# A gated cross-attention layer on one core: two batches' keys and queries built ahead of the batch loop

## The reference, cut to what matters

```python
# x: (8, 112, 256)   ctx: (8, 375, 256)   16 heads of 16 channels   8 zones, top 3
def attention(queries, keys, values, mask):          # keys = values = ctx
    q, k, v = heads(queries @ Wq + bq), heads(keys @ Wk + bk), heads(values @ Wv + bv)
    scores = where(mask, -1e15, q @ k.T / sqrt(16))
    return (softmax(scores) @ v) @ Wo + bo

def ffn(x):
    w = top-3 shares of softmax(tanh(mean_rows(x) @ W1 + b1) @ W2 + b2)    # per batch
    return x + sum over zones e of w[e] * (gelu(x @ Wa[e]) @ Wb[e])        # Wa: 256x1024, Wb: 1024x256

x = x + tanh(g_xattn) * attention(layernorm(x), ctx, ctx, mask)
x = x + tanh(g_ffn) * ffn(layernorm(x))
```

## Time and profile before

| what | value |
|---|---|
| median of three runs | 325.48 us |
| profiled execution | 328.27 us, span on the core 326.4 us |
| PE, DVE, ACT, POOL busy | 88%, 69%, 68%, 41% of the span |
| first score tile of batch 0 (start of body -1) | 24.69 us |
| starts of bodies 0, 1, 2, 3, 4, 5 and 6 | 45.01, 65.80, 85.91, 107.63, 128.33, 148.46 and 168.74 us |
| first matmul of the zone passes | 202.44 us |

### The profile page before, as it was taken

How to read it: one execution, slowest core, us unless ns; L and a number is a source line. 1 busy time by engine, 2 the same in 40 slices (tenths; PEclk the granted TensorE clock), 3 DMA queues, 4 the chain that set the end, 5 groups by cost and what they waited for, 6 DMA issues and landing times.

```text
span 326.4 us, 10356 instructions
## 1 busy us (share of the span) xinstructions
PE 287.3 (88%) x3940; PEld 238.6 (73%) x3940; DVE 225.3 (69%) x642; ACT 223.1 (68%) x439; POOL 135.4 (41%) x185
## 2 busy tenths in 40 slices
PE   1808769899989999999998977899999999999996
PEld 1505546667756776767765646799999989999996
DVE  7326846657757797777867626876976877686773
ACT  2221456786958968789687674986866977766863
POOL 3401274876768968689677983000100000000000
PEclk9967989999999999999999999999999999999999
DMA  7457667686777778866686322100201011010101
GB/s 166 120 125 239 156 176 213 167 241 172 233 182 216 206 230 230 264 177 172 207 217 208 88 87 80 38 19 16 58 17 46 3 44 37 11 45 3 32 2 30
DMA packets 39457, 40.59 MB, mean 124 GB/s; under 512 B 10264, under 2 KB 35264, under 8 KB 39408
## 3 DMA queue, kind: packets, MB, share of 16 engines
q1 hardware_dynamic: 37296, 38.94, 42.5%
q10 hardware_dynamic: 1936, 0.79, 1.0%
q0 software_dynamic: 176, 0.20, 0.2%
HBM read 33.09 MB, written 6.74 MB: 122 GB/s over the span
## 4 chain that ended last, share of the span: by engine, by line
PE 63%; DMA 12%; ACT 7%; issue 6%; DVE 5%; SPq 4%; POOL 3%; DVEq 0%; ACTq 0%
PE bank L1280 16%; PE bank L1307 16%; PE bank L1119 7%; PE bank L1128 5%; PE bank L1069 4%; DMA qbd<-q_scr 4%; PE bank L1081 4%; DMA stage<-in_L_ffn_Wb 4%; PE bank L1085 3%; PE bank L1101 2%; ACT pT L555 2%; PE bank L1110 2%; PE bank L1145 2%; DMA ctx_s<-in_ctx 2%; POOL wa L474 1%
## 5 line engine op out<-in xcount | busy, mean ns | idle before, releaser
L807 DVE CUSTOM_DVE_ANT_0 bank<-bank,maskb 112x375 f32<-112x375 f32 x128 | 67.9, 571 | 42.1 <-PE bank L1069 42.1
L1280 PE MATMUL bank<-ctxT,wqkvo 128*128 128x112 f16 x960 | 59.4, 213 | 2.7 <-DVE qbd L933 2.3
L1280 PEld LDWEIGHTS bank<-ctxT,wqkvo 128*128 128x128 f16 x960 | 56.5, 98 | 3.4 <-issue 3.4
L1307 PE MATMUL bank<-stage,pT 128*128 128x112 f16 x1104 | 58.1, 213 | 0.0
L1307 PEld LDWEIGHTS bank<-stage,pT 128*128 128x128 f16 x1104 | 55.8, 98 | 0.3
L555 ACT ACTIVATE pT<-bank 125x448 f32<-125x448 f32 x96 | 49.0, 540 | 9.9 <-PE bank L1085 9.3
L469 POOL TENSOR_SCALAR stage<-stage 128x512 f32<-128x512 f32 x64 | 38.5, 620 | 27.4 <-DMA stage<-in_L_ffn_Wa 20.6
L1069 PE MATMUL bank<-kst,qbd 128*112 128x375 f16 x128 | 33.7, 338 | 16.0 <-DMA qbd<-q_scr 12.7
L474 POOL TENSOR_TENSOR wb<-stage,wb 128x512 f16<-128x512 f32 x32 | 37.6, 1195 | 14.5 <-ACT wb L665 14.4
L1081 PE MATMUL bank<-rq,maskb 115*128 115x448 bf16 (+1 forms) x96 | 35.5, 370 | 8.3 <-ACT pT L555 7.8
L474 POOL TENSOR_TENSOR wa<-stage,wa 128x512 f16<-128x512 f32 x32 | 36.4, 1158 | 10.8 <-ACT wa L665 10.8
(11 more groups left out here) (134 smaller groups left out, 480.2 us busy)
## 6 DMA issues: line engine op xcount, KB each, us to landing
stage<-in_L_ffn_Wa SPq DMA_DIRECT2D x16, 512.0 KB, 4.5
stage<-in_L_ffn_Wb SPq DMA_DIRECT2D x16, 512.0 KB, 4.5
kst<-k_scr SPq DMA_DIRECT2D x64, 93.8 KB, 3.6
k_scr<-wb SPq DMA_DIRECT2D x16, 187.5 KB
ctx_s<-in_ctx SPq DMA_DIRECT2D x8, 336.0 KB
qbd<-q_scr SPq DMA_DIRECT2D x32, 56.0 KB, 3.0
xa<-in_x SPq DMA_DIRECT2D x8, 112.0 KB, 4.1
q_scr<-wb SPq DMA_DIRECT2D x16, 56.0 KB, 3.3
```

What stands on the lines that cost most here:

```text
L807: v.tensor_tensor_reduce(out=bank[0:SQ, e, 0:SK], in0=bank[0:SQ, e, 0:SK], in1=maskb[0:SQ, b % 2, 0:SK], scale=-1.0, scalar=FLOOR, op0=ALU ...
L1280: ins = T.matmul(o, first(ws, t, f), x2b[:, b % 2, (xs * DT + t) * SQ:(xs * DT + t + 1) * SQ], start=(t == 0 and xs == 0 and ws == 0), sto ...
L1307: ins = T.matmul(o, second(u, ws * (2 * CHUNK) + f * D + t * 128), hT[:, u % 2, hs * FT * SQ + f * SQ:hs * FT * SQ + (f + 1) * SQ], start= ...
```

## The change

- The loop starts at b = -1. What the first body did, and what the second did for batch 1, stands ahead of the loop as straight code on every engine: contexts, keys and queries of batches 0 and 1 and the values of batch 0, in the order of the tuple `AHEAD` on PE. Body -1 then holds only the score maxima of batch 0.
- In body 0 the first `s1(1, 0)` stands ahead of `st_tile(0, 0, 0)`; in all others it stays behind.
- The queries of batches 0 and 1 are read back over POOL's queue (`read_q` takes the engine), and signal semaphores of their own.
- Of the small inputs and weights that ACT's queue loaded, the key and query biases go to SP's, Wo, bv and the gates to POOL's; Wk is asked for ahead of Wq. On ACT the scaling of Wq moves behind the first copies. Two of DVE's five memsets move to POOL.
- The 64 parts of the zones' weights are spread otherwise: none ahead of body 0 slot 1, two a slot from there on, four in slot 2 of bodies 2 and 4, the last two in slot 2 of body 7.
- PE makes 12 products that nothing reads at its start and two more behind XT of batch 0 (`busy`).

```diff
--- before.py
+++ after.py
@@ parts_at
-            n = min(2 if (i, j) >= (-1, 2) else 0, NPART - at)
+            n = min(0 if (i, j) < (0, 1) else 4 if (i, j) in ((2, 2), (4, 2)) else 2, NPART - at)
@@
+def made(b):
+
+    return b + 2 if b >= 0 else B
+
+
+AHEAD = (("CX0", 0), ("CX1", 0), ("XT", 0), ("K0", 0), ("Q", 0), ("K1", 0), ("V0", 0), ("V1", 0),
+         ("CX0", 1), ("CX1", 1), ("XT", 1), ("K0", 1), ("Q", 1), ("K1", 1))
@@ slot_uses
-    n, m, o = b + 1, b + 2, b - 1
+    n, m, o = b + 1, made(b), b - 1
...
-    more = {(B - 2, 3): ("H", 0), (B - 1, 0): ("L", 0), (B - 1, 2): ("W", 0), (-1, 3): ("BO", 0)}.get((b, slot))
-    return [u for u in every[slot] if there(u[1])] + ([more] if more else [])
+    more = {(B - 2, 3): ("H", 0), (B - 1, 0): ("L", 0), (B - 1, 2): ("W", 0), (0, 3): ("BO", 0)}.get((b, slot))
+    return [u for u in every[slot] if there(u[1]) and u not in AHEAD] + ([more] if more else [])
@@ sync
+            sp.dma_start(bk_c[:, :], bk.rearrange("(t p) -> p t", p=128), allow_slow_non_contiguous=True).then_inc(s["bk_loaded"], 16)
...
+            load_mask(0)
+            load_ctx(1)
+            load_x(1)
+            write_k(0, 0)
+            write_q(0)
+            write_k(0, 1)
+            read_k(0, 0)
+            load_mask(1)
+            read_k(0, 1)
+            write_k(1, 0)
+            write_q(1)
+            load_x(2)
+            write_k(1, 1)
+            load_ctx(2)
+            read_k(1, 0)
+            for b in range(-1, B):
+                n, m, o = b + 1, made(b), b - 1
+                if n > 1:
+                    read_k(n, 1)
+                    read_q(sp, n, 1)
...
+                if b == -1:
+                    read_k(1, 1)
                 read_k(m, 0)
-                read_q(m, 0)
+                read_q(sp, m, 0)
@@ gpsimd
-            pool.wait_ge(s["zeroed"], 5)
+            chain.link(g.memset(vp[:].rearrange("p a c h i -> p (a c h i)"), 1.0))
...
+            g.memset(pT[96:CK + 1, :, :], 1.0).then_inc(s["ones_ready"], 1)
+            pool.wait_ge(s["ones_ready"], 3)
+            norm1(1)
+            read_q(pool, 0, 0)
+            read_q(pool, 0, 1)
+            g.dma_start(wqkvo[:, 3, :, :], view_w(Wo)).then_inc(s["wo_loaded"], 16)
...
+            read_q(pool, 1, 0)
+            read_q(pool, 1, 1)
+            for b in range(-1, B):
@@ scalar
             normed(0)
+            cx_copy(0)
+            xt_copy(0)
             act.wait_ge(s["wq_loaded"], 16)
...
+            k_hi(0, 0)
+            q_hi(0)
+            k_hi(0, 1)
+            v_copy(0, 0)
+            normed(1)
+            v_copy(0, 1)
+            cx_copy(1)
+            xt_copy(1)
+            mask_bias(0)
+            k_hi(1, 0)
+            q_hi(1)
+            k_hi(1, 1)
+            mask_bias(1)
@@ vector
-            v.memset(pT[96:CK + 1, :, :], 1.0).then_inc(s["zeroed"], 1)
-            dve.wait_ge(s["zeroed"], 5)
...
+            cx_copy(0)
+            dve.wait_ge(s["bk_loaded"], 16)
+            k_lo(0, 0)
...
+            ln1_stats(1)
+            cx_copy(1)
+            k_lo(1, 0)
+            q_lo(1)
+            k_lo(1, 1)
@@ tensor
+            def busy(n):
+
+                for i in range(n):
+                    T.matmul(bank[:, ST_BANKS[i % 2], 0:128], ident[:, :], ident[:, :], start=True, stop=True)
...
-            pe.wait_ge(s["zeroed"], 3)
-            for b in range(-2, B):
+            busy(12)
+            for name in AHEAD:
+                put(name)
+                if name == ("XT", 0):
+                    busy(2)
+            for b in range(-1, B):
                 for slot in range(4):
-                    st_tile(b, slot, 0)
-                    s1(b + 1, 2 * slot)
+                    if (b, slot) == (0, 0):
+                        s1(1, 0)
+                        st_tile(0, 0, 0)
+                    else:
+                        st_tile(b, slot, 0)
+                        s1(b + 1, 2 * slot)
```

More of the change, by code:

```diff
@@ L92, in __init__ @@
     def __init__(self):
-        names, banks = [], []
-        for b in range(-2, B):
+        names = list(AHEAD)
+        banks = [MISC_BANKS[i % len(MISC_BANKS)] for i in range(len(AHEAD))]
+        for b in range(-1, B):
             for slot in range(4):
@@ L284, in full, with read_q @@
             eng.wait_ge(s["misc_full"], spare.full(name))
+        def read_q(eng, b, h):
+            if there(b):
+                eng.wait_ge(s["q_written"], b * 32 + 32)
+                need(eng, s["pe_st"], tile(b - 2, 2 * h + 2, 0))
+                need(eng, s["dve_max"], s1_no(b - 2, 4 * h + 4, 0))
+                run = PAIRS * SQ
+                for e in range(2):
+                    eng.dma_start(qbd[64 * e:64 * e + 64, b % 2, e, HP * h:HP * h + HP, :].rearrange("p j f -> p (j f)"),
+                                 bass.AP(q_scr.tensor, (b * DT + e) * (HD * 2 * run) + HP * h * SQ,
+                                         [[run, 2 * HD], [0, 2], [1, HP * SQ]])).then_inc(s["q_first%d%d" % (b, h)] if b < 2 else kq_in[b % 2][h], 16)
         block = stack.enter_context(nc.Block())
@@ L319, in write_k @@
                                  k_hl[:, t, :, :]).then_inc(k_written[t], 16)
-            def read_q(b, h):
-                if there(b):
-                    sp.wait_ge(s["q_written"], b * 32 + 32)
-                    need(sp, s["pe_st"], tile(b - 2, 2 * h + 2, 0))
-                    need(sp, s["dve_max"], s1_no(b - 2, 4 * h + 4, 0))
-                    run = PAIRS * SQ
-                    for e in range(2):
-                        sp.dma_start(qbd[64 * e:64 * e + 64, b % 2, e, HP * h:HP * h + HP, :].rearrange("p j f -> p (j f)"),
-                                     bass.AP(q_scr.tensor, (b * DT + e) * (HD * 2 * run) + HP * h * SQ,
-                                             [[run, 2 * HD], [0, 2], [1, HP * SQ]])).then_inc(kq_in[b % 2][h], 16)
             def read_k(b, h):
@@ L536, in _ @@
             a = nc.scalar
+            a.dma_start(wqkvo[:, 1, :, :], view_w(Wk)).then_inc(s["wk_loaded"], 16)
             a.dma_start(wq_in, view_w(Wq)).then_inc(s["wq_loaded"], 16)
[L538 to L545 removed]
             def exp_tile(b, g, c):
@@ L679, in _ @@
             normed(0)
+            cx_copy(0)
+            xt_copy(0)
             act.wait_ge(s["wq_loaded"], 16)
             a.activation(wq_p[:, :, :, :], wq_in.rearrange("p k (t j i) -> p (k t) i j", t=DT, i=HD), ACT.Copy, scale=HD ** -0.5).then_inc(s["wq_scaled"], 1)
-            for b in range(-2, B):
-                n, m, o = b + 1, b + 2, b - 1
+            act.wait_ge(s["bq_loaded"], 32)
+            a.activation(bq_c[:, :], bq_c[:, :], ACT.Copy, scale=HD ** -0.5).then_inc(s["wq_scaled"], 1)
+            act.wait_ge(s["wq_scaled"], 2)
+            act.wait_ge(s["bk_loaded"], 16)
+            k_hi(0, 0)
[11 more added lines that the diff above has]
+            mask_bias(1)
+            for b in range(-1, B):
+                n, m, o = b + 1, made(b), b - 1
                 exp_tile(b, 0, 0)
@@ L1093, in pv @@
                     pe.wait_ge(s["act_exp"], tile(b, g, 2) + 1)
+                    if b == 0 and g == 0:
+                        pe.wait_ge(s["zeroed"], 2)
                     if g == 0:
```

67 lines of the change are left out of this document (30 added, 37 removed).

## The result

The changed kernel takes 341.76 us (median of 4 runs, 338.88 to 343.21); in the same comparison the kernel before took 325.62 us (4 runs, 325.46 to 326.13). The ratio is 1.048 with an interval of 1.041 to 1.055: slower. The profiled execution took 341.29 us for a span of 339.4 us, 13.0 us more than the 326.4 of before.

What follows compares the result with a forecast made beforehand. PE was taken to bound the bodies with nothing to spare, SP's queue running just in time. Terms -12.5 + 20.0 + 2.0 + 0.5 = +10.0 us gave 338.3 profiled, 335.5 us as median; range 327.5 to 342.

Steps and rivals of the forecast that it cites:

- The start: Straight code ahead of the loop: body 0 starts at 32.1 instead of 45.01; 12.5 us gained, bounds 9.5 to 14.5.
- The four-part slots: Bodies 2 and 4, four parts in slot 2: POOL and SP wait on loads; 20.0 us lost together.
- A's low halves: POOL's low halves of slot 0's pair of parts; their end, 6.8 us into body 4, starts the count.
- D: Second pair of slot 2's four parts; its load waits for A's low halves and lands 4.5 us after them.
- E: Slot 3's pair of parts; SP can load it only after 8.1 us of the count, and it lands at 12.7.
- C's low halves: POOL's low halves of slot 2's first pair; they end at 16.9 us of the count, before SP's next reads.
- The clock: PE's clock falls after the two new stops, in the bodies behind them: 2.0 us lost, between 0 and 3.3.
- The end: Body 7: the last pair comes a slot later and delays the first zone's weights; 0.5 us, between 0 and 2.
- From the span to the median: Whole kernel: the profiled execution, forecast at 338.3 us, lies 2.8 us above the median, so 335.5.
- slack in the ring: Rival, bodies 2 and 4: POOL has room and the weights' loads hide; 313.5 us, faster; chance 0.09.
- half a stall: Rival, bodies 2 and 4: loads come near 3 us, each body loses 5 to 6; 324 to 327 us; chance 0.07.
- little gain of the straight code: Rival, ahead of the loop: late keys or queries start body 0 at 38; 341.5 to 342 us; chance 0.06.

Runs made afterwards that it cites:

- the experiment: Changed kernel with SP's write of batch 1's second keys put ahead of the load of batch 2's x; 340.59 us, ratio 1.045.
- the stagger: Changed kernel with the same parts, but loads and scalings of bodies 2 and 4 asked for one place later; 325.79 us, ratio 1.000.
- the old spread: Changed kernel with weights' parts spread as before: two a slot from body -1 slot 2 on, none with four; 324.81 us, ratio 0.995.
- the second experiment: Kernel before with nothing but the new spread of the weights' parts; 347.25 us, ratio 1.065.

## Why the prediction was right

The forecast was slower, 335.5 us with a range of 327.5 to 342; 341.76 lies at the very top of the range, and outside the 330 to 341 that the forecast's own bounds gave. The mechanism held in every link, and sizes were off in most terms.

- **The start** (-12.5): measured -11.14. Body -1 began at 20.65, 1 us earlier than forecast, but took 13.2 instead of 10.4 us, as batch 1's keys came at 33.8, not 31.6; PE stood 1.56 us for them, so the maxima were ready by 32.3, near the forecast's 32.1. SP's second write was late by its stop at the load of x (1.1 us by the experiment) and took 5.40, not 4.29.
- **The four-part slots** (+20.0): measured +7.51 and +9.59, 17.1. From T, the end of A's low halves, the steps of body 2 came at 4.6 (D is scaled; forecast 4.5), 8.2 (E asked for; 8.1), 12.4 (E is scaled; 12.7), 16.5 (C's low halves end; 16.9) and 22.5 (the next body starts; 23.4); those of body 4 at 4.2, 7.9, 11.7, 15.8 and 23.0. T was 6.8 us behind the start in both. The forecast for body 2 had averaged this case (8.5) with a later T; the nearer one was right. The Trainium skill's fit of 2.0 us plus the bytes over 436 GB/s ("DMA: Bandwidth & Descriptors", anatomy of one DMA) gave 15, an estimate; the Trainium skill's page measured it on DMAs over GpSimd's queue, and these go over SP's. The four loads that count landed 3.8 to 4.5 us after their issue, so the trace's price was the better one. PE's own waits for the queries, 6.06 and 7.42 us, were shorter than the 10 that were named as a sign; they are the largest part of the 9.25 and 9.68 us that PE is idle in these two bodies.
- **The clock** (+2.0): bodies 3 and 5 lost 1.35 and 1.43, together 2.8 us, inside its bounds.
- **The end** (+0.5): measured +3.05, outside its bound of 2. The last pair itself costs 0.4 to 0.7 us: bodies 6 and 7 take 34.15 us in the stagger, which has the same parts, against 33.70 before, both at a mean clock of 1.00, and 34.83 and 34.86 without the unread products and with the write ahead against 34.15 and 34.19 with the old spread, all at 0.95. The rest goes with PE's clock, which in the changed kernel's trace (mean 0.91) fell behind a wait of 1.68 us for `wdiag`: a pair of products (line 1145) takes 0.58 instead of 0.36 us until the zones begin. I had not looked for a wait there. Traces with the same parts differ by 2.6 us here; what decides how long the clock stays down is open.
- **Body 1** (+0, "so nothing"): +1.16. The read of queries landed 4.55 us after its issue and PE waited 1.00 us. The queue that runs just in time has no cover in that body.
- **From the span to the median** (-2.8): measured +0.5. The forecast took off what the profile of before lay above its median. The changed kernel's profiled execution took 341.29 us, 3.0 above the forecast's 338.3, and its median is 341.76. So of the 6.3 us between 335.5 and 341.76, 3.3 come from this step.

Some of the agreement is luck: the two stalls came out 2.9 us smaller than forecast, the other terms of the profiled execution 5.9 us larger together, so half of that was hidden.

What the prediction did not see at all lies beside it. First, that the gain and the loss are one trade: with the old spread the earlier start is worth only 0.5% (0.0 to 1.0), since body 0's weights then come late (28.54 us for that body). Second, the path by POOL's norm1 to ACT, which would have held the next body about as long as the queries did. It ended 0.4 us behind the landing of the queries in body 2 and 0.8 us behind it in body 4, so leaving it out cost the count little only because the two paths are about equally long; that is luck too.

Of the rivals, slack in the ring and half a stall are refuted by the 7.51 and 9.59 us that bodies 2 and 4 lost and by the second experiment; little gain of the straight code by body 0's start at 33.87. How the 11.14 us of the start split is shown only in part: the unread products are 2.1 of them. No run takes out the reads over POOL's queue, the moved memset or the first score tile ahead of `st_tile`.

## What to carry to other kernels

A ring shared by an in-order loader and an in-order consumer has slack only in the order written: doubling one slot's work made POOL wait twice for a load that it had itself just set free, with SP's writes and reads behind it, 9 and 11 us a time with the body behind each, while the same work asked for one place later cost 1.7 and 3.3. Before moving work out of a start-up phase, ask where it goes and which transfers it then meets; before mending one queue, look what stands behind the same event on the others.
